# Layer 3's spreads as four 32-row tiles with hats in rows of four, made sooner, and layer 1's deviation by logarithm and exponential

## The reference, cut to what matters

```python
py = base_y + ky + dy; px = base_x + kx + dx
samp = bilinear(x, py, px) * mask          # (B, C, 9, H, W)
out = einsum("bckhw,ock->bohw", samp, weight) + bias
```

```python
mu = mean(y, axis=-1); var = mean(square(y - mu), axis=-1)
y = (y - mu) * rsqrt(var + 1e-5) * ln_g + ln_b
out = einsum("bld,od->blo", y, W_out)
```

## Time and profile before

| | us |
|---|---|
| median of the runs (three) | 551.65 |
| lowest, highest | 547.44, 551.67 |
| the profiled execution, its own time | 542.76 |
| its span, first to last instruction | 541.0 |
| layer 1's quads and tail | 130 to 204 |
| layer 3, from its norm to the first spread | 358 to 401 |
| layer 3's 72 steps and the last add | 401 to 536 |

### The profile page before, as it was taken

The page is one execution under the profiler, slowest core; times in us unless marked ns, Lnnn a source line. Parts: engine busy times, 40 slices in busy tenths (PEclk is TensorE's granted clock), DMA queues, the critical chain, the costliest instruction groups (busy, mean ns, idle before and its releaser), DMA issues. The chain is left out here.

```text
span 541.0 us, 9049 instructions
## 1 busy us (share of the span) xinstructions
PE 408.6 (76%) x3218; PEld 207.1 (38%) x3218; DVE 355.1 (66%) x670; ACT 289.2 (53%) x509; POOL 119.2 (22%) x138
## 2 busy tenths in 40 slices
PE   1325681499999736488999999938269999999995
PEld 1114561245555413323333333325125544455442
DVE  4547786313365696988999998150446878788784
ACT  1459974113223413417888888812737668486441
POOL 4500003100000001864431111010004618156000
PEclk9856986599999985958999999977759999999998
DMA  5300000720000000882210000008674290742302
GB/s 138 116 0 1 0 0 0 146 48 1 0 1 0 1 0 1 233 274 81 80 41 3 4 2 2 2 22 180 155 158 105 52 213 2 175 89 63 70 2 78
DMA packets 21496, 34.35 MB, mean 64 GB/s; under 512 B 5376, under 2 KB 16336, under 8 KB 20688
## 3 DMA queue, kind: packets, MB, share of 16 engines
q1 hardware_dynamic: 17488, 24.94, 19.5%
q10 hardware_dynamic: 2688, 4.16, 3.2%
q0 software_dynamic: 1280, 4.72, 3.0%
HBM read 16.80 MB, written 4.64 MB: 40 GB/s over the span
## 5 line engine op out<-in xcount | busy, mean ns | idle before, releaser
L1259 DVE TENSOR_TENSOR L_s<-L_row_ps,L_cols 128x1024 f32<-128x1024 f32 x72 | 87.7, 1219 | 8.3 <-PE L_row_ps L1390 6.7
L877 DVE TENSOR_REDUCE L_mx<-L_ring 128x2 f32<-128x512 f32 x128 | 83.3, 687 | 10.4 <-PE L_ring L1000 9.9
L932 ACT ACTIVATE L_e<-L_ring 128x512 f32<-128x512 f32 x128 | 73.6, 597 | 20.9 <-PE L_ring L1013 18.9
L1411 PE MATMUL L_acc<-L_s,L_t_sb 128*64 128x256 f32 x576 | 79.8, 399 | 1.1 <-DVE L_s L1259 1.0
L1320 ACT ACTIVATE L_cols<-L_col_ps 128x512 f32<-128x512 f32 x72 | 42.8, 596 | 44.7 <-PE L_col_ps L1398 44.2
L1000 PE MATMUL L_ring<-stacks_k_st,stacks_q_st 64*128 64x256 bf16 x256 | 50.7, 300 | 7.0 <-DVE L_v_all L866 5.5
L1411 PEld LDWEIGHTS L_acc<-L_s,L_t_sb 128*64 128x64 f32 x576 | 35.5, 138 | 35.1 <-DVE L_s L1259 21.2
L1013 PE MATMUL L_ring<-stacks_q_st,stacks_k_st 64*128 64x256 bf16 x256 | 47.0, 281 | 1.7 <-DMA stacks_q_st<-L_m_parts 1.7
L1390 PE MATMUL L_row_ps<-L_hats,L_sel 48*128 48x512 bf16 x144 | 44.5, 391 | 0.0
L1033 PE MATMUL L_ctx_ps<-L_e,L_v_x 128*32 128x256 f32 x512 | 40.7, 391 | 0.0
L1381 PE MATMUL L_acc<-all_w_all,L_xn 64*128 64x192 f32 x96 | 26.3, 356 | 13.9 <-DVE L_t_sb L1239 13.9
(11 more groups left out here) (254 smaller groups left out, 765.4 us busy)
## 6 DMA issues: line engine op xcount, KB each, us to landing
L_hats<-L_parts SPq DMA_DIRECT2D x32, 216.0 KB, 5.0
L_hat<-L_offsets SPq DMA_DIRECT2D x24, 192.0 KB, 4.5
L_mask<-L_offsets SPq DMA_DIRECT2D x12, 192.0 KB, 4.6
stacks_q_st<-L_q_parts SPq DMA_DIRECT2D x12, 128.0 KB, 3.7
stacks_k_st<-L_k_parts ACTq DMA_DIRECT2D x12, 128.0 KB, 5.1
stacks_q_st<-L_q_parts POOLq DMA_DIRECT2D x12, 128.0 KB, 2.7
stacks_k_st<-L_k_parts POOLq DMA_DIRECT2D x12, 128.0 KB, 3.0
L_stack<-L_xpad SPq DMA_DIRECT2D x8, 162.0 KB, 5.7
```

Source lines behind the costliest of these rows:

```text
L877: dve.tensor_reduce(mx[:, n % 2, :, head], ring[:, place(step) % 3].rearrange("p (q s) -> p q s", q=2), AX.X, ALU.max).then_inc(max_read, 1)
L932: act.activation(e[:, k], ring[:, 3 + v % 3], ACT.Exp, scale=HD2 ** -0.5).then_inc(e_ready, 1)
L1259: dve.tensor_tensor(s[:, q], row_ps[:, q], cols[:, t % 3:t % 3 + 1].broadcast_to([P, 2, 2 * N]), ALU.mult).then_inc(s_ready, 1)
L1411: mm = pe.matmul(acc[C * e:C * e + C, b, 0:N], t_sb[:, b, h, (KK * e + t) * C:(KK * e + t + 1) * C], s[:, q, h, e * N:(e + 1) * N], start= ...
```

## The change

In layer 3:
- Each hat takes four rows in place of three, the fourth zero, so that eight positions fill 32 rows. `parts` gets a fourth part, cleared once by POOL. The places of an image are reordered (`by_place`), so that half of the places needs only eight of the sixteen columns.
- `spread_rows` issues two matmuls on rows 0 to 31 and 32 to 63, with 128 columns. `spread_cols` issues two on rows 64 to 95 and 96 to 127, with 64 columns each, into the two halves of one bank of `col_ps`.
- `hat` and `mask` get two buffers, `hats` four. Loads go out as soon as their buffer is free, in part ahead of the hats' transfers.
- Chunk 1's hat steps lie in steps 0 to 7 of the loop, chunk 2's in 15 to 26, chunk 3's in 33 to 44 (before: 0 to 11, 18 to 29, 36 to 47).
- The loops of SP and POOL are written out, not run by a register.
- `norm` on ACT, and the first two images' on DVE, are two instructions of 128 columns each.

In layer 1 the deviation's reciprocal is `exp(-0.5 * ln(var))` on ACT, with the table set named ahead, and DVE's reciprocal goes. In layers 0 to 2 the private step semaphores become one shared one.

```diff
 # layer 1
                 def over_deviation(q):
 
                     dve.wait_ge(sd_ready, q + 1)
-                    dve.reciprocal(sd[:], sd[:]).then_inc(scaled, 1)
-                    dve.wait_ge(scaled, 2 * q + 1)
                     dve.tensor_tensor(sd[:], o[:], sd[:], ALU.mult).then_inc(scaled, 1)
-                    dve.wait_ge(scaled, 2 * q + 2)
+                    dve.wait_ge(scaled, q + 1)
...
                 def deviation(q):
+                    act.preload_act_table_set("natural_log_exp_and_others")
                     act.wait_ge(o_copied, 2 * q + 4)
-                    act.activation(sd[:], var[:], ACT.Sqrt).then_inc(sd_ready, 1)
+                    act.activation(lnvar[:], var[:], ACT.Ln).then_inc(ln_ready, 1)
+                    act.wait_ge(ln_ready, q + 1)
+                    act.activation(sd[:], lnvar[:], ACT.Exp, scale=-0.5).then_inc(sd_ready, 1)
 # layer 3
-        sel = m.sb("sel", [P, 3, P], BF16)
+        sel = m.sb("sel", [P, P], BF16)
-        hat, mask = m.sb("hat", [P, TN]), m.sb("mask", [C, TN])
-        rest, parts = m.sb("rest", [P, 2, THIRD]), m.sb("parts", [P, 3, TN], BF16)
-        hats = m.sb("hats", [P, 2, 2, TN], BF16)
+        hat, mask = m.sb("hat", [P, 2, TN]), m.sb("mask", [C, 2, TN])
+        rest, parts = m.sb("rest", [P, 2, THIRD]), m.sb("parts", [P, 4, TN], BF16)
+        hats = m.sb("hats", [P, 4, 2, TN], BF16)
...
-                def send_hats(b):
+                def load_chunk(c, j):
+                    sp.wait_ge(hat_in[j], 32 * c)
+                    sp.wait_ge(mask_in[j], 16 * c)
+                    if c > 1:
+                        sp.wait_ge(parts_ready, 3 * c - 3)
+                    load_positions(c, j)
+                    load_masks(c, j)
+
+                def send_hats(n):
+                    sp.wait_ge(parts_ready, 3 * (n // 2) + 3)
+                    if n > 3:
+                        sp.wait_ge(s_used, KK * (n - 3) + 2)
                     for k in range(2):
                         for e in range(2):
-                            first = C * k + 2 * b + e
-                            sp.dma_start(hats[C * k:C * k + 3 * H, b, e, :], parts[first:C * k + C:CH]).then_inc(hats_in[b], 16)
-
-                def next_chunk(i, more):
-                    sp.wait_ge(parts_ready, 3 * i + 6)
-                    for b in range(2):
-                        sp.wait_ge(s_used, KK * (2 * i + b) + 10)
-                        send_hats(b)
-                        if more and b == 0:
-                            for j in range(3):
-                                load_positions(i + 2, j)
-                                load_masks(i + 2, j)
+                            first = C * k + 2 * (n % 2) + e
+                            sp.dma_start(hats[C * k:C * k + C, n % 4, e, :], parts[first:C * k + C:CH]).then_inc(hats_in[n % 4], 16)
...
-                sp.wait_ge(parts_ready, 3)
-                send_hats(0)
-                send_hats(1)
                 sp.wait_ge(off_stored, 128)
                 sp.wait_ge(mask_stored, 128)
-                for j in range(3):
-                    load_positions(1, j)
-                    load_masks(1, j)
-                with sp.Fori(0, B // CH - 2) as i:
-                    next_chunk(i, True)
-                next_chunk(B // CH - 2, False)
+                sp.wait_ge(edge_ready, 3)
+                load_chunk(1, 0)
+                send_hats(0)
+                load_chunk(1, 1)
+                send_hats(1)
+                load_chunk(1, 2)
+                for c in range(2, B // CH):
+                    for j in range(3):
+                        load_chunk(c, j)
+                    for n in range(2 * c - 2, 2 * c):
+                        send_hats(n)
+                for n in range(NP - 2, NP):
+                    send_hats(n)
...
                 pad_stack(pool, edge_ready, xpad, stack)
+                pool.wait_ge(edge_ready, 2)
+                pool.memset(parts[:, 3, :].bitcast(F32), 0.0).then_inc(edge_ready, 1)
...
-                        h = KK * (n % 2) + t
-                        if n < NP - 2 and h < len(hat_steps):
+                        for later, h in hats_of_step(KK * n + t):
                             hat_step, j = hat_steps[h]
-                            hat_step(n // 2 + 1, j)
+                            hat_step(later, j)
...
                     for h in range(2):
-                        mm = pe.matmul(row_ps[:, v % 2, h], sel[0:3 * H, h], hats[0:3 * H, n % 2, :, t * N:(t + 1) * N], start=True, stop=True)
+                        rows = slice(32 * h, 32 * h + 32)
+                        mm = pe.matmul(row_ps[:, v % 2, h], sel[rows, :], hats[rows, n % 4, :, t * N:(t + 1) * N], start=True, stop=True)
...
                     pe.wait_ge(col_read, c - 1)
-                    pe.matmul(col_ps[:, c % 2], sel[C:C + 3 * H, 2], hats[C:C + 3 * H, n % 2, :, t * N:(t + 1) * N],
-                              start=True, stop=True).then_inc(col_ready, 1)
+                    for a in range(2):
+                        rows = slice(C + 32 * a, C + 32 * a + 32)
+                        mm = pe.matmul(col_ps[C * a:C * a + C, c % 2], sel[rows, 0:C], hats[rows, n % 4, :, t * N:(t + 1) * N], start=True, stop=True)
+                    mm.then_inc(col_ready, 1)
...
+def hats_of_step(step):
+    found = [(1, h) for h in range(12) if 2 * h // 3 == step]
+    return found + [(c, step - first) for c, first in ((2, 15), (3, 33)) if 0 <= step - first < 12]
```

More of the change, by code:

```diff
@@ L279, in _ @@
                 dve.sem_inc(norm1_ready, 1)
-                step = Steps(dve, own)
+                step = Steps(dve, signals.own, signals.own_steps)
                 dve.wait_ge(h2_ready, 1)
@@ L316, in _ @@
                 step(dve.tensor_tensor(zc0[:], zc0[:], c0[:], ALU.add))
+                signals.own_steps = step.n
                 with dve.Fori(0, NP // 2) as i:
@@ L1122, in weigh_hat @@
                 eng.wait_ge(mask_in[j], 16 * c + 16)
-                eng.tensor_tensor(hat[0:C, cut], hat[0:C, cut], mask[:, cut], ALU.mult).then_inc(masked, 1)
+                eng.tensor_tensor(hat[0:C, c % 2, cut], hat[0:C, c % 2, cut], mask[:, c % 2, cut], ALU.mult).then_inc(masked, 1)
             def take_rest(c, j):
@@ L1130, in take_rest @@
                 eng.wait_ge(hi_ready, 3 * c + j + 1)
-                eng.tensor_tensor(rest[:, j % 2], hat[:, cut], parts[:, 0, cut], ALU.subtract).then_inc(rest_ready, 1)
+                eng.tensor_tensor(rest[:, j % 2], hat[:, c % 2, cut], parts[:, 0, cut], ALU.subtract).then_inc(rest_ready, 1)
             def take_last(c, j):
@@ L1217, in _ @@
                 pad_stack(pool, edge_ready, xpad, stack)
-                with pool.Fori(1, B // CH) as c:
+                pool.wait_ge(edge_ready, 2)
+                pool.memset(parts[:, 3, :].bitcast(F32), 0.0).then_inc(edge_ready, 1)
+                for c in range(1, B // CH):
                     for hat_step, j in hat_split(pool):
@@ L1303, in take_first @@
                     act.wait_ge(masked, 3 * c + j + 1)
-                    if from_turn(c, 1):
-                        for b in range(2):
-                            act.wait_ge(hats_in[b], 64 * c)
-                    act.activation(parts[:, 0, cut], hat[:, cut], ACT.Copy).then_inc(hi_ready, 1)
+                    if c:
+                        for n in range(2 * c - 2, 2 * c):
+                            act.wait_ge(hats_in[n % 4], 64 * (n // 4 + 1))
+                    act.activation(parts[:, 0, cut], hat[:, c % 2, cut], ACT.Copy).then_inc(hi_ready, 1)
                 def take_second(c, j):
@@ L1328, in norm @@
                     act.wait_ge(col_ready, 15 * n - 23)
-                    act.activation(xn[:, n % 2, :], x[:, n, :], ACT.Identity, scale=gn.scale[:, n:n + 1], bias=gn.shift[:, n:n + 1]).then_inc(xn_ready, 1)
+                    for a in range(2):
+                        act.activation(by_place(xn[:, n % 2, :], a), by_row(x[:, n, :], a), ACT.Identity, scale=gn.scale[:, n:n + 1],
+                                       bias=gn.shift[:, n:n + 1]).then_inc(xn_ready, 1)
                 hat_steps = ((take_distance, 0), (make_hat, 0), (take_distance, 1), (make_hat, 1), (take_first, 0), (take_distance, 2),
@@ L1533, in lay_out @@
     t["l3_vec"] = np.stack([np.tile(np.pad(bias, (0, 32 - 27)), 4), -(part % C // 4).astype(f), np.tile(a["L3_conv_bias"], 2)], 1)
-    k, r = np.divmod(part, 3)
-    col = part[None, :]
-    rows = [(part[:, None] < 48) & (k[:, None] == 8 * h + col // W) for h in range(2)]
-    k = (part - 64) // 3
-    t["sel"] = np.stack(rows + [(part[:, None] >= 64) & (part[:, None] < 112) & (k[:, None] == col % W)], 1).astype(f)
+    place = np.arange(P)
+    row, row_part = np.divmod(part % 32, 4)
+    y_of, x_of = place[None, :] // 8 % 8, place[None, :] % 8
+    t["sel"] = ((row_part[:, None] < 3) & (row[:, None] == np.where(part[:, None] < C, y_of, x_of))).astype(f)
     tap_y, tap_x = np.divmod(np.arange(9), 3)
```

44 lines of the change are left out of this document (26 added, 18 removed).

## The result

The changed kernel is slower: 562.53 us as the median of four runs (554.75 to 568.14), against 549.55 us for the kernel before (four runs, 542.24 to 551.67). The ratio is 1.021, with a 95% interval from 1.012 to 1.031, so the change costs 1.2 to 3.1%. The ratio leaves out two slower executions of the changed kernel (568.14 and 564.07 us, both at a lower granted clock), so it is not the quotient of the two medians. The forecast was 563.4 us. Its difference, +11.7 us, is also what the ratio gives on 549.55 us (0.0212 x 549.55 = 11.7, by the interval 6.4 to 16.9); the two medians differ by 13.0. The profiled execution took 560.99 us with a span of 559.2, where before's took 542.76 with 541.0.

What follows compares the result with a forecast made beforehand. Layer 3's 72-step loop was taken as bound by TensorE. Terms 16.0 - 4.1 + 0.3 + 1.2 - 1.7 = +11.7 us on the median 551.65 gave 563.4 us, whole range 540 to 572, likeliest case 556 to 571.

Steps and rivals of the forecast that it cites:

- The stays: Layer 3's spreads: row and column pairs take two separate stays, steps of 2.18 and 1.65 us, +16.0 us; chance 0.50.
- The step that carried the forecast: Layer 3's spreads: any change of tile shape, even of width alone, makes all the array pay; upper bound taken, +16.0 us.
- The hats: Layer 3, images 2, 4 and 6: hats made earlier end PE's three waits of 1.36 us, -4.1 us.
- Chunk 1's early steps: Layer 3, steps 0 to 7: twelve hat steps on ACT hold column copies behind a wait for POOL, 0.3 us (0 to 2).
- Supply and ACT together: Layer 3's loop: waits for hats gone, -4.1 us, plus 0.3 us charged for early hat steps on ACT.
- The loop in all: Layer 3's loop: 16.0 for two stays, -4.1 for the waits, 0.3 for ACT's early hat steps.
- The start of the loop: Before layer 3's first spread: hat transfers with a third more bytes land later, +1.2 us (0 to 1.7).
- Layer 1: Layer 1's tail: logarithm and exponential on ACT replace the square root and DVE's reciprocal, -1.7 us; hidden in the quads.
- the case with the smaller gain: Layer 1's tail: the table load of 1.28 us is repeated, -1.7 us; if it isn't, -3.0.
- One bank: Layer 3: column tiles sharing a bank take turns, 0.216 us a step; 579 us (0.10), or 555.8 without two stays (0.08).
- One turn after all: Layer 3: all four spreads start together on disjoint rows, steps of 1.86 and 1.37 us; -10.1, 541.6 us; chance 0.32.
- The hats stay late: Layer 3: hats still late through ACT's queue or fuller DMAs, up to 4 + 2 us on any case; no separate chance.

Runs made afterwards that it cites:

- width experiment: Kernel before, with the column spread issued as two tiles of 64 columns in place of one of 128, on the same rows: 581.21 us in one run.
- on 64 rows: Changed kernel with before's 64x128 spreads, keeping four-row hats, the earlier supply and layer 1's change: 548.16 us, no verdict against before's 545.93.
- one-shape kernel: Changed kernel with each row spread as two tiles of 64 columns, so all six spreads are 32x64: 538.41 us, ratio 0.988 to the kernel before.
- layer 1 alone: Kernel before with only layer 1's deviation by logarithm and exponential: 545.03 us in one run, beside 550.47 for before.
- version to keep: one-shape kernel with three layer 1 edits on ACT (table loads, tail's logarithm earlier): 538.01 us, ratio 0.980 to before; 0.982 in a second set.
- late hats: The kernel on 64 rows with the hat steps back at 0, 18 and 36, buffers and SP's order still changed: 545.22 us in one run.

## Why the prediction was right

**The stays** were sized within 0.02 us each: 2.19 and 1.67 measured, 2.18 and 1.65 forecast. The step that carried the forecast, that tiles of another width drain the array even on disjoint rows, had no row of its own and had been read off tiles that overlap. The width experiment shows it directly. At the same supply the new tiles cost 14.6 us (16.0 forecast). The kernel that this is taken against, on 64 rows, loses 0.6 us to chunk 1's early hats and 0.4 to a lower clock in image 0, and the changed one loses neither, so the tiles' own cost is nearer to 15.6.

The Trainium skill (TensorEngine Tiling (Array Packing), Key Properties) says that a change of the tiling mode drains TensorE and that a change of tile alone does not. Both halves agree with the runs: 0.31 us between pairs of unlike width (0.53 behind two turns), 0.02 among six tiles of one form. It gives no price, which here was 0.10 to 0.13 us over the turns for bf16.

**The hats.** No wait of PE for them is left, as forecast. Before's three even images were longer by 1.53, 1.48 and 1.31 us, 4.3 in all (4.1 forecast). Chunk 1's early steps cost 0.3 us by the prediction; the kernel on 64 rows shows 0.6. In the changed kernel this is hidden: image 1 takes 18.15 us like the later ones, presumably since PE's longer steps leave ACT the time. Supply and ACT together are -3.1 us at the old step (-3.5 without image 0's clock), for a forecast of -3.8.

That the waits are gone from the changed kernel is not, by itself, the earlier making's doing. The width experiment has before's supply and no wait for hats: at 20.09 us an image, the hats of images 2, 4 and 6 landed 1.1 to 1.3 us before the column spread that needs them. Before, at 15.95 us an image, they came some 1.5 us too late. A straight line between the two (an estimate) puts the old supply at about zero at the change's 18.15 us, where the new one has 4.9 to 5.1 us to spare. So the slower steps alone would have removed nearly all of the waits, and the new supply earns its 3 us only with steps as short as before's or shorter. The prediction added the two terms as if they were independent; its sum holds because the waits go either way.

**The loop in all:** +11.5 us measured, 16.0 - 4.1 + 0.3 = +12.2 forecast.

**The start of the loop** was put too high: +1.2 forecast. From DVE's last piece of the hats to the first spread it is 8.23 us before and 8.71 after, so +0.5. The transfers of `hats` grew by a third, but their median time from issue to landing only from 5.0 to 5.1 us. Most of the 0.5 us lies in the issue: the fourth transfer goes out 2.27 us behind the first, before it was 1.90. SP's row of the first transfers and PE's row of the first spread:

```profile
398.13 3.61 SPq L1196 DMA_DIRECT2D L_hats<-L_parts  x4
```

```profile
405.86 0.63 PE L1421 MATMUL L_col_ps<-L_hats,L_sel 32*64 32x512 bf16 x2 [0.61 <-ACT L_t_sb L1341]
```

The page names ACT's copy as releaser, and the fourth transfer landed at 405.62 us, 0.24 before the spread, as it did before (400.91 and 401.15). Both still end together.

**Layer 1** came out as forecast: -1.8 us for -1.7. The table load stands in the tail, as the case with the smaller gain had it. ACT's timeline, and DVE's product behind it:

```profile
201.44 1.28 ACT L599 ACT_TABLE_LOAD   x1 [2.56 <-DVE all_x L534]
202.73 0.63 ACT L601 ACTIVATE L_lnvar<-L_var 128x512 f32<-128x512 f32 x1
203.39 0.63 ACT L603 ACTIVATE L_sd<-L_lnvar 128x512 f32<-128x512 f32 x1
```

```profile
204.05 0.69 DVE L528 TENSOR_TENSOR L_sd<-L_o,L_sd 128x512 f32<-128x512 f32 x1 [1.85 <-ACT L_sd L603]
```

Load, logarithm, exponential and product follow each other with gaps of 0.01 to 0.03 us. The Trainium skill (ScalarE: Activation LUTs, What ACT_TABLE_LOAD costs) adds a drain of 1.38 us to a load of 1.28, 2.66 in all. The load agrees; the drain does not show here, where ACT was idle ahead of the load and went on 0.01 us behind it. The page speaks of a switch to another set, and this load names a set that is active already. But at such a switch, behind a busy ACT, the drain doesn't show either: in the kernel before a silu ends at 183.94, the load follows at 183.96 and the square root at 185.26 us.

```profile
182.93 1.01 ACT L605 ACTIVATE L_zs<-L_z_ps 128x1024 f32<-128x1024 f32 x1
...
185.26 0.63 ACT L598 ACTIVATE L_sd<-L_var 128x512 f32<-128x512 f32 x1
```

With the drain, by an estimate from that page's figure, the tail would have gained 0.4 us in place of 1.8.

**The rivals.** "One bank" predicted column tiles 0.22 us apart; both start in the same merged row, within 0.01 us, and the six of the one-shape kernel start within 0.02. "One turn after all" needed all four within 0.02 us: 0.31 were measured. "The hats stay late" needed a wait that isn't there.

**What the two spans differ by beyond that.** The forecast asked for +11.7 us, and the profiled executions differ by 18.2. The loop has 11.5. At the first spread the changed one was 4.7 us late already, and the end has 1.9.
- By the norm behind layer 1 it was 2.2 late. 0.9 of that stood by the third quad's centering, 0.7 of it already at the norm ahead of layer 1; in the last quad and the tail the lower clock of the last section costs 1.5 each, and the edit gives back 1.8.
- By layer 3's norm it was 3.2 late. From there to the first spread it took 44.74 us, 1.5 more than the 43.21 of before's trace. But the two experiments whose layer 3 is before's up to there (width, layer 1 alone) took 44.87 and 44.86, so it is rather before's trace that was short there.
- The end is the transfer of the output: from its issue to the end of the span 4.9 us before, 6.8 here, and 4.9 again in all eight other traces. It belongs to this one execution.

How much the stretch ahead of the loop varies, two kernels show that were traced twice: their first spreads came at 401.07 and 411.56 us (one shape), and at 406.23 and 397.68 (the version to keep). The other edits of the change (norms in two instructions, the shared semaphore, loops written out) have no run of their own, and what they cost or give would not be seen beside that.

Loop, start of the loop and layer 1 add up to 11.5 + 0.5 - 1.8 = +10.2 us as measured, for +11.7 forecast. The mechanism of each term is as told. That the median came within 0.9 us of 563.4 is in part luck: before's own median moved by 2.1 us with a fourth run, and the interval on the difference is 6.4 to 16.9 us.

## What to carry to other kernels

Count the tile shapes in a step before counting the tiles: each change of shape costs a stay of its own, on disjoint rows too and also where only the width differs, so work that should overlap has to be issued in one form, if need be in more and smaller tiles. Here two additional matmuls per step turned a loss of 2% into a gain of 1%. When transfers are waited for, make their input sooner first and look at buffers after that, and price the early work by the steps beside which it will lie: here it cost 0.6 us beside steps of 1.87 us and nothing beside steps of 2.19. And a wait that faster supply removes may go by itself when the steps get longer: do not count it twice.

## What the runs showed of the hardware

The granted TensorE clock in the last quad and the tail of layer 1 differs between executions of one and the same kernel. These are the windows of that stretch (columns as above; the clock is third from the end): the kernel before, the changed one, and the width experiment, whose layer 1 is the kernel's before.

```profile
186.00:200.00 14.00, 6.43 (x43) 3.17 (x32) 11.39 (x13) 1.66 (x2) 0.00 (x0) 1.00 0.00 0
```

```profile
186.00:200.00 14.00, 9.86 (x44) 4.96 (x44) 5.09 (x8) 2.45 (x4) 0.00 (x0) 0.76 0.00 0
```

```profile
186.00:200.00 14.00, 9.74 (x44) 4.80 (x41) 8.64 (x10) 1.08 (x2) 0.00 (x0) 0.76 0.00 0
```

PE starts as many matmuls in each window and is busy half as long again at 0.76. In the same window one execution of the one-shape kernel had 0.99 and another 0.64; the final version 0.76 and 0.87; the kernel on 64 rows 0.60, with late hats 1.00; layer 1's edit alone 0.86. The changed kernel's layer 1 is the one-shape kernel's, instruction for instruction. Its last quad, from the centering before to its own, took 17.81 us where the other's took 16.27, and its tail 12.32 where the other's took 10.81 (the same twenty matmuls busy for 5.70 us against 4.08), so the clock cost it 3.0 us in all. In the one-shape kernel's second execution it was 4.4 us (18.49 and 12.97). What sets the clock there I haven't found.
